# Long attention by residue classes, and sets of one job for jobs 14 and 15

## The reference

```python
x = x + 0.5 * ffn(layernorm(x), ...)
x = x + attn(layernorm(x))
x = x + 0.5 * ffn(layernorm(x), ...)

def attn(x):                       # r = 4, segments of 64
    xs = x.reshape(B, g, seg, r, D)          # position p = i*4 + offset
    scores = einsum('bgqrd,bgkrd->brgqk', xs, xs) * scale
    probs = softmax(scores)
    return einsum('brgqk,bgkrd->bgqrd', probs, xs).reshape(B, S, D) / r

def ffn(x, ...):                   # 16 heads of 8, causal; E = 8 experts, 2 per token
    h = layernorm(x + causal_attention(x) @ w_o, g1, b1)
    w = the two largest softmax(h @ wg), scaled to sum 1, else 0
    h1 = gelu(einsum('bsd,edf->ebsf', h, w1) + bb1)      # F = 512
    y = einsum('ebsf,efd->ebsd', h1, w2) + bb2
    return layernorm(h + einsum('ebsd,bse->bsd', y, w), g2, b2)
```

## Time and profile before

| what | value |
|---|---|
| median of 3 runs | 1218.78 us (1218.28 to 1222.53) |
| profiled execution | 1228.96 us, span 1227.1 us |
| mean granted clock of TensorE | 0.893 |
| busy: TensorE, VectorE, ScalarE, GpSimd | 1042.0, 693.5, 655.5, 586.3 us |
| HBM read, written | 145.10 MB, 38.68 MB |
| DMAs of the SyncE queue, GpSimd's | 162.32 MB, 16.79 MB |

### The profile page before, as it was taken

How to read it: one execution, slowest core, us unless ns; L and a number is a source line. 1 busy time by engine, 2 the same in 40 slices (tenths; PEclk the granted TensorE clock), 3 DMA queues, 4 the chain that set the end, 5 groups by cost and what they waited for, 6 DMA issues and landing times.

```text
span 1227.1 us, 29800 instructions
## 1 busy us (share of the span) xinstructions
PE 1042.0 (85%) x10977; PEld 837.6 (68%) x10977; DVE 693.5 (57%) x2452; ACT 655.5 (53%) x1478; POOL 586.3 (48%) x711
## 2 busy tenths in 40 slices
PE   4888979998989989898989979898899988776660
PEld 3566647886867777686767867787777866676660
DVE  6548656563568745685558835786557723520413
ACT  1233425774666656675656746666566747343240
POOL 2224455236555545546464555656364466443415
PEclk9878979997989988898988989999889979888685
DMA  4492116655545646544555545545456546576561
GB/s 80 97 210 60 37 35 171 196 164 147 155 151 133 187 117 171 137 124 162 147 145 156 159 127 148 161 147 172 127 158 174 169 138 180 165 247 221 169 213 45
DMA packets 116471, 181.01 MB, mean 148 GB/s; under 512 B 12360, under 2 KB 79464, under 8 KB 116328
## 3 DMA queue, kind: packets, MB, share of 16 engines
q1 hardware_dynamic: 108136, 162.32, 46.9%
q0 software_dynamic: 8192, 16.79, 4.8%
HBM read 145.10 MB, written 38.68 MB: 150 GB/s over the span
## 4 chain that ended last, share of the span: by engine, by line
PE 72%; DVE 8%; another core or an unknown queue 6%; issue 6%; ACT 5%; POOL 2%; DMA 1%; POOLq 0%; ACTq 0%; DVEq 0%
PE ps_ring L569 15%; PE ps_ring L578 12%; PE ps_quad L440 8%; PE ps_quad L473 6%; PE ps_quad L469 6%; PE ps_ring L486 5%; PE ps_quad L446 3%; PE ps_ring L490 2%; ACT probs L653 2%; PE ps_ring L413 2%; PE ps_ring L501 2%; PE ps_ring L560 2%; PE ps_ring L420 1%; POOL picked L1107 1%
## 5 line engine op out<-in xcount | busy, mean ns | idle before, releaser
L1045 POOL TENSOR_SCALAR_AFFINE_SELECT probs<-probs 128x512 f32<-128x512 f32 x256 | 178.7, 707 | 272.2 <-ACT probs L653 265.9
L653 ACT ACTIVATE probs<-ps_quad 128x768 f32<-128x768 f32 x256 | 194.0, 806 | 162.5 <-PE ps_quad L473 100.6
L689 ACT ACTIVATE act<-ps_ring,weights 128x128 f32<-128x128 f32 x736 | 201.8, 385 | 123.9 <-PE ps_ring L569 90.1
L816 DVE TENSOR_REDUCE shift_cols<-ps_quad 128x2 f32<-128x512 f32 (+3 forms) x256 | 149.9, 586 | 153.5 <-PE ps_quad L454 117.8
L578 PE MATMUL ps_ring<-weights,act 128*128 128x128 f32 x1472 | 202.3, 286 | 35.1 <-ACT act L689 18.8
L569 PE MATMUL ps_ring<-tile_t,weights 128*128 128x128 f32 x1472 | 199.6, 293 | 17.0 <-ACT tile_t L680 8.8
L578 PEld LDWEIGHTS ps_ring<-weights,act 128*128 128x128 f32 x1472 | 185.1, 199 | 38.5 <-ACT act L689 20.6
L569 PEld LDWEIGHTS ps_ring<-tile_t,weights 128*128 128x128 f32 x1472 | 185.7, 205 | 31.1 <-issue 18.3
L1107 POOL DMA_INDIRECT picked<-sorted_outputs,place x128 | 123.2, 962 | 81.9 <-issue 81.6
L941 DVE TENSOR_TENSOR tile_y<-ps_ring,weights 128x128 f32<-128x128 f32 x184 | 51.1, 287 | 191.8 <-PE ps_ring L578 97.5
L1094 POOL DMA_INDIRECT sorted_rows<-h_rows,place x128 | 124.0, 969 | 52.3 <-issue 34.5
(11 more groups left out here) (132 smaller groups left out, 1532.2 us busy)
## 6 DMA issues: line engine op xcount, KB each, us to landing
weights<-expert_weights SPq DMA_DIRECT2D x184, 578.0 KB
tile_rows<-sorted_rows SPq DMA_DIRECT2D x56, 192.0 KB
sorted_outputs<-tile_y SPq DMA_DIRECT2D x56, 192.0 KB
query_key_parts<-qk SPq DMA_DIRECT2D x32, 256.0 KB, 4.8
k<-query_key_parts SPq DMA_DIRECT2D x64, 64.0 KB
q<-query_key_parts SPq DMA_DIRECT2D x64, 64.0 KB
sorted_rows<-zeros SPq DMA_DIRECT2D x2, 1472.0 KB, 10.7
xs<-in_L_attn_x SPq DMA_DIRECT2D x8, 256.0 KB, 5.6
```

What stands on the lines that cost most here:

```text
L653: sc.activation(probs[:, r % PROBS, 2 * a:2 * a + 2, :], ps_quad[:, 2 * a:2 * a + 2, 0:3 * P], ACT.Exp, scale=HD ** -0.5).then_inc(pair_fr ...
L689: ins = sc.activation(act[:, k % ACTS, f, :], bank(use)[:, f * P:(f + 1) * P], ACT.Gelu_apprx_tanh, bias=weights[:, k % WEIGHTS, 2 * F + f ...
L816: dve.tensor_reduce(shift_cols[:, late, groups], ps_quad[:, groups, 0:split], AX.X, ALU.max)
L1045: pool.affine_select(out=both, in_=both, compare_op=ALU.is_ge, fill=0.0, base=0, pattern=[[0, 2], [0, 2], [1, P]], channel_multiplier=-1). ...
```

## The change

1. A chunk's rows are held by position modulo four: partition 64 g + n of group h holds position 4n + 2h + g. Loads and stores of x are cut into four DMAs per chunk for it. The causal attention and the projections need the tokens in order, so ScalarE writes the transposed rows (`turn`) back into the order of the positions, and `merge` back into that of the remainders. In the long attention a row group then holds two whole classes of 64: the scores are made only within a row group, the exponential only for the two 64 x 64 blocks (the others stay zero from the start), the values from one key tile. GpSimd's mask goes.
2. Jobs 14 and 15 are sets of their own (`JOB_SETS`), with 15 tiles each. Buffers, DRAM tables and the two waits on older sets are made for three sets under way.
3. The last job's combination goes row group by row group, each waiting for its own gathers, and subtracts the mean and scales by g2 in one step, the reciprocal deviation and the residual following in a second; job 14 has the last two steps as well. The last two sequences are stored one by one.
4. `PLACES` has new values, and the tables `EARLY`, `NEXT`, `LAST` and `LATE` override them for the first four jobs, jobs 12 and 13 (and set 7), jobs 14 and 15 (and set 8), and set 6.

```diff
-SETS = JOBS // 2
-SET_TT = 2 * TT
-TILES = (2 * SET_TT * P + E * (P - 1)) // P
+JOB_SETS = ((0, 1), (2, 3), (4, 5), (6, 7), (8, 9), (10, 11), (12, 13), (14,), (15,))
+SETS = len(JOB_SETS)
+UNDER_WAY = 3
...
+def tiles_of(s):
+    return (2 * rows_of(s) * P + E * (P - 1)) // P
...
+    "scores0": -1.927, "scores1": -1.378, "exps0": 0.315, "exps1": 0.823, "weigh0": 1.451, "weigh1": 1.679,
...
+    slots, apart, free = {}, at(PLACES, "apart"), 0
+    for s, jobs in enumerate(JOB_SETS):
+        phase = EARLY if s == 0 else LAST if s == SETS - 1 else NEXT if s == SETS - 2 else LATE if s == SETS - 3 else {}
+        pace = at(phase, "pace")
+        known = 4 * jobs[-1] - 4
+        begin = max(known, free)
+        free = begin + pace * batches_of(s)
+        done = begin + pace * (batches_of(s) - 8)
...
+            slot = slots[m] = max(done + c, slots[m - 2] + apart if m >= 2 else 0)
...
-    x_tiles = x.rearrange("(c q) (h p) d -> c p (q h) d", q=2, p=P)
-    out_tiles = out.rearrange("(c q) (h p) d -> c p (q h) d", q=2, p=P)
+    x_phases = x.rearrange("(c q) (n h g) d -> c g n q h d", q=2, h=2, g=2)
+    out_phases = out.rearrange("(c q) (n h g) d -> c g n q h d", q=2, h=2, g=2)
...
-            sp.dma_start(xs[:, 0:TT, :], x_tiles[0]).then_inc(x_in[0], 16)
+            def load_chunk(c):
+                for g in range(2):
+                    for q in range(2):
+                        sp.dma_start(xs[PHASE * g:PHASE * g + PHASE, TT * c + 2 * q:TT * c + 2 * q + 2, :],
+                                     x_phases[c, g][:, q, :, :]).then_inc(x_in[c], 16)
+
+            load_chunk(0)
...
-                for i in range(2):
+                for i in range(UNDER_WAY):
                     sp.dma_start(sorted_h[i].rearrange("(t p) d -> p t d", p=P),
-                                 zeros[:, :].unsqueeze(1).broadcast_to([P, TILES, D])).then_inc(zeroed, 16)
+                                 zeros[:, :].unsqueeze(1).broadcast_to([P, SORTED[i], D])).then_inc(zeroed, 16)
...
+            def store_sequence(c, q):
+                for g in range(2):
+                    sp.dma_start(out_phases[c, g][:, q, :, :],
+                                 chunk_rows(c)[PHASE * g:PHASE * g + PHASE, 2 * q:2 * q + 2, :]).then_inc(stored, 16)
+
             def store(c):
+                if CHUNKS + c == JOBS - 1:
+                    for h in range(2):
+                        sp.wait_ge(last_result, h + 1)
+                        store_sequence(c, h)
+                    return
                 sp.wait_ge(result_ready, CHUNKS + c + 1)
-                sp.dma_start(out_tiles[c], chunk_rows(c)).then_inc(stored, 16)
+                for q in range(2):
+                    store_sequence(c, q)
...
-                    mm = pe.matmul(bank(use)[:, kt * S:(kt + 1) * S],
-                                   long_xn_t[:, b * S + kt * P:b * S + (kt + 1) * P],
-                                   long_xn_t[:, b * S:(b + 1) * S], start=True, stop=True)
+                    both = long_xn_t[:, b * S + kt * P:b * S + (kt + 1) * P]
+                    mm = pe.matmul(bank(use)[:, kt * P:(kt + 1) * P], both, both, start=True, stop=True)
...
-                pe.wait_ge(long_masked, 2 * c + b + 1)
+                freed(pe, ("long_scores", c, b))
                 take(pe, use)
                 for qt in range(2):
-                    for kt in range(2):
-                        mm = pe.matmul(bank(use)[:, qt * S:qt * S + D + 1],
-                                       long_e[:, b, kt, qt * P:(qt + 1) * P], long_xn[:, 2 * b + kt, 0:D + 1],
-                                       start=(kt == 0), stop=(kt == 1))
+                    mm = pe.matmul(bank(use)[:, qt * S:qt * S + D + 1], long_e[:, b, qt, :],
+                                   long_xn[:, 2 * b + qt, 0:D + 1], start=True, stop=True)
...
-                sc.activation(xn_t[:, :], bank(("turn", m)), ACT.Copy).then_inc(free_sem(("turn", m)), 1)
+                sc.activation(xn_t[:, :].rearrange("p (q n r) -> p q r n", q=2, r=RATE),
+                              bank(("turn", m)).rearrange("p (q r n) -> p q r n", q=2, r=RATE), ACT.Copy
+                              ).then_inc(free_sem(("turn", m)), 1)
...
-                sc.activation(long_e[:, b, :, :].rearrange("p k q -> p (k q)"), bank(use), ACT.Exp, scale=D ** -0.5
-                              ).then_inc(free_sem(use), 1)
+                pairs = bank(use)[:, 0:S].rearrange("p (k q) -> p k q", k=2)
+                for r in range(2):
+                    at = slice(PHASE * r, PHASE * r + PHASE)
+                    ins = sc.activation(long_e[at, b, :, at], pairs[at, :, at], ACT.Exp, scale=D ** -0.5)
+                ins.then_inc(free_sem(use), 1)
...
+            def combine_last():
+                m = JOBS - 1
+                first, second = picked[:, m % 2, 0, :, :], picked[:, m % 2, 1, :, :]
+                for tt in range(TT):
+                    dve.wait_ge(last_rows_in[tt], 32)
+                    step(dve.scalar_tensor_tensor(out=first[:, tt, :], in0=first[:, tt, :],
+                                                  scalar=gates[:, m % 8, 0, tt:tt + 1], in1=h_rows[:, m % KEPT, tt, :],
+                                                  op0=ALU.mult, op1=ALU.add))
+                    settle()
+                    step(dve.scalar_tensor_tensor(out=first[:, tt, :], in0=second[:, tt, :],
+                                                  scalar=gates[:, m % 8, 1, tt:tt + 1], in1=first[:, tt, :],
+                                                  op0=ALU.mult, op1=ALU.add))
+                    settle()
+                    step(dve.bn_stats(stats[:, END, tt, :], first[:, tt, :]))
+                    settle()
+                    step(dve.bn_aggr(moments[:, END, tt, :], stats[:, END, tt, :]))
+                    settle()
+                    if tt < TT - 1:
+                        dve.scalar_tensor_tensor(out=first[:, tt, :], in0=first[:, tt, :],
+                                                 scalar=moments[:, END, tt, 0:1], in1=g2_half[:, :],
+                                                 op0=ALU.subtract, op1=ALU.mult)
+                dve.tensor_scalar(var_eps[:, END, :], moments[:, END, :, 1], EPS, None, ALU.add
+                                  ).then_inc(var_ready[END], 1)
+                step(dve.scalar_tensor_tensor(out=first[:, TT - 1, :], in0=first[:, TT - 1, :],
+                                              scalar=moments[:, END, TT - 1, 0:1], in1=g2_half[:, :],
+                                              op0=ALU.subtract, op1=ALU.mult))
...
+            def finish_last():
+                m = JOBS - 1
+                rows = picked[:, m % 2, 0, :, :]
+                dve.wait_ge(residual_ready, m + 1)
+                settle()
+                dve.wait_ge(rstd_ready[END], m + 1)
+                for tt in range(TT):
+                    out_rows = chunk_rows(m)[:, tt, :]
+                    ins = dve.scalar_tensor_tensor(out=out_rows, in0=rows[:, tt, :], scalar=rstd[:, END, tt:tt + 1],
+                                                   in1=out_rows, op0=ALU.mult, op1=ALU.add)
+                    if tt % 2:
+                        ins.then_inc(last_result, 1)
...
-                m = 2 * s + t // TT
+                        pool.wait_ge(tile_y_out[par], 16 * outputs(s - UNDER_WAY, par))
+                m = JOB_SETS[s][t // TT]
...
+                landed = last_rows_in[tt] if m == JOBS - 1 else gathered[m % 2]
...
-            def long_scores(c, b):
-                freed(pool, ("long_scores", c, b))
-                pairs = long_e[:, b, :, :].rearrange("p k (n r) -> p (k n) r", r=RATE)
-                pool.tensor_tensor(pairs, pairs,
-                                   phase_of[:, :].unsqueeze(1).broadcast_to([P, 2 * S // RATE, RATE]), ALU.mult
-                                   ).then_inc(long_masked, 1)
```

331 lines of the change are left out of this document (203 added, 128 removed), and 24 rows, old and new, of tables (EARLY, LAST, LATE, PLACES).

## The result

The changed kernel took 1237.22 us (median of four runs, 1232.72 to 1240.12) beside 1219.52 us of the kernel before on the same chip: ratio 1.0138, 95% interval 1.0096 to 1.018. 1202 us was forecast, and the range ended at 1221. The profiled execution took 1239.76 us, 10.8 more than that of before.

The account below looks back on a forecast made before the run. TensorE was taken to set the pace in the body, before a 142 us tail. Terms -16 + 3 - 2 + 15 - 5 + 7 - 3 - 15.6 = -16.6; 1229.0 - 16.6 - 10.2 gave 1202 us, own range 1193 to 1212, with rivals 1184 to 1221.

Parts of the forecast that it names:

- three signs of being wrong: Periods keeping their 143 us, a tail from the last rank longer than 145 us, or a finish over 28.
- first rival: Body: the new places there pay as well, 2.5 us in each of six periods, giving 1187 us; chance 0.20.
- The long attention: Body: shorter score and value products save 1.11 us for each of 16 sequences, 17.7 us; -16 taken.
- The start: Loading x in quarters, the last 1.5 us later, and half of 3.5 us for clearing a third buffer: +3 us.
- The finish: Last tile result to the end: eight gathers instead of 16 and shorter row steps, 38.6 to 23.0 us, saving 15.6.
- Seven more tiles: Tail: 191 tiles instead of 184, at 2.13 us each, cost +15 us.
- Job 14's scatters: Eight scatters move from the tail (0.96 us each) into the last attention (0.75 each); -2 us taken.
- The fourth rival: Tail bound by indirect DMAs, 1227 us; decided if tiles beside job 14's gathers need over 4 us; chance 0.13.
- Job 12's and 13's combination: Tail: job 12's combination two tiles later shortens VectorE's 5.47 us wait for gathered rows; -5 us, job 13 included.
- Job 15's turn: Three more tiles' first products stand before TensorE's 4.74 us wait for job 15's rows; -3 us.
- the second (the saving vanishes): Long attention: a wait takes the place of the saved matmuls, so 1218 us, no change; chance 0.13.
- the third: Start and last two stores: quarter transfers land one after the other, +7 and +3 us, so 1212; chance 0.09.

Follow-up runs that it names:

- the pair on one chip: The changed kernel (1.0208) and the changed kernel with `expand` back from -2.639 to -2.689 (1.0011), ratios to the kernel before at 1071 us.
- expand_late_again: old_sets_order with `expand` moved from -2.689 to -2.639, rerun where the kernel before takes 1220.09 us: ratio 1.0067.
- residual_later: expand_late_again with GpSimd's residual addition moved from 1.522 to 2.2, kernel before at 1220.09 us: ratio 0.9906.
- rows_alone: Changed kernel with the sets, order and finish of before, leaving only rows by position modulo four: ratio 0.9879 to the kernel before.
- old_sets_order: Changed kernel with the sets and order of before, keeping new rows and new finish: ratios 0.9853, 0.9856 and 0.9815 to the kernel before.
- whole_loads: old_sets_order with each chunk of x loaded in one DMA, rows in plain order: ratio 0.9833 to the kernel before.
- the kernel with the old places: Changed kernel with the four tables emptied and the `PLACES` of before, new sets kept: ratio 0.9977 to the kernel before.
- late_scatters: The kernel with the old places, job 14's eight scatters moved on GpSimd behind job 15's rows: ratio 0.9933 to the kernel before.

## Why the prediction was wrong, step by step

- **The size of the miss.** By the profiled executions it is 27.4 us (1239.76 against 1229.0 - 16.6): 9.1 at the start, 6.2 in the body, 8.4 in the last attention, 3.6 in the tail. The other 7.7 us of the 35 come from the difference carried over: before's profiled execution lay 10.2 us above its median, the changed kernel's 2.5. None of the three signs of being wrong appeared (the fourth and fifth periods take 139.2 and 137.7 us, the tail 139.4, the finish 22.4): they watched the places that had a large term. The last rank, expected 10 us before 1085, came at 1098.6.
- **The middle's places: the step that failed.** The prediction gave them no term, and set aside the first rival's mechanism with "the places of the middle jobs move by hundredths of a half". Five hundredths turned two pieces of VectorE's queue round, 14 times. Where the kernel before takes 1070 us this costs 2.0% by the pair on one chip, 2.5 to 3.1% by the others. Where it takes 1220 us, the six body periods take 812.6 us before, 810.2 in `expand_late_again` and 795.6 in `residual_later`, where the expansion no longer meets the addition: -2.4 and -17.0, beside the -16 of the prediction. So there the swap, through that overlap as far as the runs tell, took about what the long attention saved. The first measurement has the wait too: in the changed kernel TensorE's idle time before these scores that VectorE's reductions end is 20.5 us, before 14.6. It is probably why the body shows -9.8 and not -16; no kernel without the swap was timed at 1220 us.
- **The long attention: right.** `rows_alone` gives 0.9879, -12.9 us at 1068.63 (-17.7 to -8.1 by the interval), against -16 + 3 = -13. Its periods are 3.7 us shorter (4.4 was the most that the products save). GpSimd's mask and ScalarE hid as assumed, although the permuted copies do take 1.09 and 1.08 us instead of 0.60: 15 us more of ScalarE, beside TensorE.
- **The start: +3 was +12.1, and its parts are not separated.** The quarters are as forecast: VectorE's first row statistics come 1.7 us later (5.44 against 3.73), and at 5.06 in `old_sets_order` against 3.89 in `whole_loads`. A quarter lands in 2.3 us (median of 32), and the next is issued long before that. The Trainium skill, SBUF — State Buffer, "The DMA setup-cost knee", states about 2 us for each DMA; the +6 that I worked out from it, an estimate for quarters in series, does not show, so here they overlap. The clearing was mis-sized: SyncE spends 12.22 us on three buffers and 6.96 on two, so 5.3 more and not 3.5; whether TensorE waits for it was not tried apart. The clock is lower up to the first rank, 0.84 against 0.88, which is 28.0 against 19.6 us of lost work. The swap has a part as well, but not the whole: at 1070 us the first rank came at 167.6 us on average in five profiles with it (163.8 to 171.4) and at 161.5 in eleven without (157.4 to 168.8); at 1220 us it came at 164.6 in `expand_late_again`, only 1.5 later than before.
- **The finish: right**, 22.4 us against 23.0, and in its parts too: the code is worth 4.7 us and the eight gathers fewer 11.2 (of 4.1 and 11.5 in the prediction's sum). With two jobs a set it is 35.4.
- **Seven more tiles, +15**, is right in count; the tail as a whole missed by 3.6 us (-2.7 against -6.3). The gap of 10.8 us between sets 7 and 8, of which 3.24 are TensorE's wait for set 8's rows, had no term. It was not tried apart.
- **Job 14's scatters: mis-sized, -2 was +5.** In the kernel with the old places they cost 7.1 us in the last attention (`late_scatters`, 97.7 to 90.6) and 0.44% of the time, by ratios from two chips; 11.4 us were lost there in the first measurement, and how much of it is theirs is not known. I priced them by GpSimd's mean over a period and did not ask what is queued behind them. The fourth rival named this place at +9 of its 25 us, and nothing for the places of the body. Its own sign is just missed: beside job 14's gathers three tiles took 3.8 us each (1180.46 to 1191.80), and it wanted over 4.
- **Job 12's and 13's combination**: the wait is 1.69 us against 5.47, near the -5. **Job 15's turn**: 0.5 us of waiting is left of 4.74, better than -3.
- The rivals: the second (the saving vanishes) was half right: it was spent, but by a swap elsewhere; the third fell with the row statistics, 1.7 us later and not 8.7; the first had the right place and the wrong sign.

So at 1070 us: -12.9 (rows) -2.8 (finish) +13.3 (sets) +32 (middle's places) -1 (tables) = +28.6, and 1.0266 is +28.4. This sum closes by construction, each part being the difference of two neighbours in the table, so its closing proves nothing. At 1220 us the total is +17.7. Which of the parts is smaller there is open, since only two kernels were timed there besides.

## What to carry to other kernels

A table that sets the order has no small entries: compare the queues, not the numbers, and price every swap by what the queue waits for behind it. When an instruction moves on VectorE or GpSimd, look at what the other of the two runs beside its new place; an instruction of 0.34 us can take 1.96 there. And take the profiled execution against the profiled execution: the distance of one of them from its median is no constant of the kernel.
